# Moving the early routed rows' scatters to other places in GpSimd's program, in the last four passes of an audio tower kernel

## What is computed

```python
h = tok_ref(x, W, b)                           # signatures @ W.T + b
h = h + attn_ref(layernorm(h), ...)
h = h + ffn_ref(layernorm(h), ...)

def ffn_ref(x, gate_w, w1, w2, w3, sw1, sw2):  # D = 128, I = 512, E = 8, K = 1
    logits = xf @ gate_w.T
    wts, idx = top_k(logits, 1)
    comb = one_hot(idx) * softmax(wts)
    h = silu(xf @ w1[e].T) * (xf @ w3[e].T)    # of each expert e
    y = sum over e of (h * comb) @ w2[e].T
    return y + gelu(xf @ sw1.T) @ sw2.T
```

## Time and profile before

| | |
|---|---|
| median of 3 runs | 676.93 us (676.33 to 677.5) |
| profiled execution, whole | 676.65 us |
| its span | 674.8 us |
| TensorE (PE) busy | 638.4 us, 95% |
| VectorE (DVE) busy | 417.5 us, 62% |
| GpSimd (POOL) busy | 298.7 us, 44% |
| ScalarE (ACT) busy | 288.2 us, 43% |
| granted clock of TensorE, mean | 0.987 |

### The profile page before, as it was taken

The page is one execution under the profiler, slowest core; times in us unless marked ns, Lnnn a source line. Parts: engine busy times, 40 slices in busy tenths (PEclk is TensorE's granted clock), DMA queues, the critical chain, the costliest instruction groups (busy, mean ns, idle before and its releaser), DMA issues.

```text
span 674.8 us, 14377 instructions
## 1 busy us (share of the span) xinstructions
PE 638.4 (95%) x4237; PEld 539.0 (80%) x4270; DVE 417.5 (62%) x1073; ACT 288.2 (43%) x656; POOL 298.7 (44%) x336
## 2 busy tenths in 40 slices
PE   5989999999999999999999999999798999999994
PEld 3767888877888788887788887778577999999994
DVE  7966666666666666665666667776535354555534
ACT  3334444544445444445444454433374433444450
POOL 1355444545445454455444454445853213333330
PEclk9989999999999999999999999999988999999997
DMA  8511433534634434334343342112335211111108
GB/s 310 220 68 33 106 78 85 116 80 101 118 78 111 92 87 101 78 92 111 78 105 82 79 114 46 36 35 69 86 91 191 64 33 38 43 44 44 46 26 250
DMA packets 70006, 61.81 MB, mean 92 GB/s; under 512 B 6092, under 2 KB 58189, under 8 KB 69600
## 3 DMA queue, kind: packets, MB, share of 16 engines
q1 hardware_dynamic: 67712, 57.31, 33.6%
q0 software_dynamic: 2272, 4.22, 1.8%
HBM read 18.88 MB, written 26.30 MB: 67 GB/s over the span
## 4 chain that ended last, share of the span: by engine, by line
PE 81%; DVE 7%; issue 4%; POOL 3%; ACT 2%; DMA 1%; SPq 1%; DVEq 0%; POOLq 0%; ACTq 0%
PE bank L1256 74%; PE bank L1312 2%; PE bank L1465 2%; POOL sorted_rows L502 1%; POOL z L487 1%; DMA x<-expert_rows 1%; SPq L432 1%; PE bank L1556 1%; PE bank L1371 1%; PE bank L1362 0%; PE bank L1317 0%; POOL z L489 0%; PE bank L1316 0%; DMA sq<-square 0%; DVE utl L796 0%
## 5 line engine op out<-in xcount | busy, mean ns | idle before, releaser
L1256 PE MATMUL bank<-whigh,uth 128*128 128x512 f32 x512 | 168.8, 410 | 1.2 <-DVE lowt L796 1.2
L1256 PEld LDWEIGHTS bank<-whigh,uth 128*128 128x128 f32 x512 | 92.2, 190 | 28.0 <-issue 7.4
L1256 PE MATMUL bank<-whigh,utl 128*128 128x512 f32 x256 | 101.8, 398 | 0.0
L496 POOL TENSOR_TENSOR rstd<-rstd,powers 128x1 f32<-128x1 f32 x64 | 35.3, 551 | 119.9 <-DVE rstd L889 64.7
L487 POOL TENSOR_TENSOR z<-z 128x512 f32<-128x512 f32 x32 | 42.3, 1322 | 91.0 <-DVE z L902 91.0
L573 POOL DMA_INDIRECT expert_rows<-prob,ids x39 | 38.3, 983 | 89.2 <-ACT prob L750 89.2
L1256 PE MATMUL bank<-xvo,x 128*128 128x128 f32 x624 | 76.4, 276 | 0.7 <-issue 0.4
L1256 PEld LDWEIGHTS bank<-xvo,x 128*128 128x128 f32 x624 | 72.8, 192 | 1.4 <-issue 0.7
L1256 PE MATMUL bank<-xT,qkw 128*128 128x128 f32 x512 | 63.7, 278 | 0.0
L1256 PEld LDWEIGHTS bank<-xT,qkw 128*128 128x128 f32 x512 | 60.8, 195 | 0.1
L1256 PEld LDWEIGHTS bank<-whigh,utl 128*128 128x128 f32 x256 | 48.3, 189 | 11.9
(11 more groups left out here) (229 smaller groups left out, 1325.9 us busy)
## 6 DMA issues: line engine op xcount, KB each, us to landing
sorted_rows<-blank SPq DMA_DIRECT2D x24, 709.5 KB, 6.3
xvp<-xvo SPq DMA_DIRECT2D x128, 128.0 KB
w<-w_t SPq DMA_DIRECT2D x1, 4096.0 KB, 12.0
xvo<-sorted_rows SPq DMA_DIRECT2D x39, 64.5 KB, 1.9
w<-w_high SPq DMA_DIRECT2D x4, 512.0 KB, 6.8
x_columns<-x2t SPq DMA_DIRECT2D x32, 64.0 KB
xg_in<-x_columns SPq DMA_DIRECT2D x8, 256.0 KB
levels<-w_t SPq DMA_DIRECT2D x1, 2048.0 KB, 7.7
```

The source lines that it names most:

```text
L496: G.tensor_tensor(rstd[:, n, 1:2], rstd[:, n, 0:1], powers[:, 0:1], ALU.pow) \
L1256: return T.matmul(out_, lhsT, rhs, start=start, stop=stop)
```

## The change

The 24 early scatters are issued in the same order, at other places of POOL's program:

| place in POOL's program | before | after |
|---|---|---|
| pass 28, last | 0 to 2 | 0 to 2 |
| pass 29, between root(0, 30) and root(1, 28) | 3 to 5 | 3 to 5 |
| pass 29, between root(1, 28) and add_channels(31) | 6, 7 | 6 |
| pass 29, behind add_channels(31), ahead of root(0, 31) | 8 to 10 | 7 |
| pass 30, between root(0, 31) and root(1, 29) | 11 to 13 | 8 to 10 |
| pass 30, behind root(1, 29) | 14 to 19 | 11 to 16 |
| pass 31, behind root(1, 30), ahead of root(1, 31) | 20 to 23 | 17 to 19 |
| behind root(1, 31), ahead of the wait for pos_ready | none | 20 to 23 |

```diff
@@ in POOL's iteration(i, f, u, acc, prev) @@
                 if is_tile(i, SCATTER_AT + 1):
                     scatter(range(3, 6))
                 if is_tile(i, SCATTER_AT + 2):
-                    scatter(range(11, 14))
+                    scatter(range(8, 11))
                 if prev:
                     root(1, ln2, i - 1)
                 if is_tile(i, SCATTER_AT + 1):
-                    scatter(range(6, 8))
+                    scatter(range(6, 7))
                 if is_tile(i, SCATTER_AT + 2):
-                    scatter(range(14, 20))
+                    scatter(range(11, 17))
                 if is_tile(i, SCATTER_AT + 3):
-                    scatter(range(20, EARLY))
+                    scatter(range(17, 20))
                 if u:
                     add_channels(i + 2)
...
                 if is_tile(i, SCATTER_AT + 1):
-                    scatter(range(8, 11))
+                    scatter(range(7, 8))
...
             iteration(TILES - 1, False, False, False)
             root(1, ln2, TILES - 1)
+            scatter(range(20, EARLY))
```

## The result

| | before | after |
|---|---|---|
| first comparison: median (runs) | 676.63 us (4) | 671.38 us (4) |
| ratio, 95% interval | | 0.9924, 0.9906 to 0.9941 |
| two later comparisons, ratio and interval | | 0.9940 (0.9919 to 0.9961), 0.9934 (0.9913 to 0.9955) |
| profiled execution, span | 676.65, 674.8 us | 670.9, 669.1 us |

The change makes the kernel faster, by 5.1 us in the first comparison and 4.1 and 4.5 in the later ones (each ratio times 676).

The account below looks back on a forecast made before the run. Bound by TensorE nearly everywhere, with POOL's early scatters delaying work that DVE or PE awaits. Gains of 0.9, 0.6, 0.8 and 0.8 make 3.1 us: 676.65 - 3.1 = 673.55, put down as 673.6, range 671.8 to 675.2.

Parts of the forecast that it names:

- sum over channels of pass 29: Pass 29 on POOL: with scatter 7 behind it, the sum starts at 476.65 in place of 477.57; gain 0.9 us.
- xn of pass 30, to the softmax product: First norm of pass 30: DVE's 1.06 us wait for the root goes, but ACT's exponential limits the gain to 0.6.
- x2n of tile 29: Second norm of pass 30: the three scatters ahead of its root start sooner, so the root starts at once; gain 0.8.
- to x2n of tile 30, forecast by the clock near 490: Stretch near 490 where ACT is the bound: with an earlier clock fall gone, 0.1 to 0.2 us.
- x2n of tile 31: Last norm, pass 31: three scatters, not four, ahead of the root cut DVE's 1.47 us wait to 0.65; gain 0.8.
- up(2)'s clock: PE's shared-expert matmuls after two idle times: half clock there costs 1.58 us, which shorter gaps might save.
- A: Main case: gains as summed, clock falling again at up(2): 3.1 us, 673.6 (673.1 to 674.6); chance 0.47.
- B: Same gains, but shorter gaps leave the clock full before up(2): 3.1 + 1.6 = 4.7 us, 672.1; chance 0.31.
- the lower bound: Pass 29's sum: gain only 0.3 us if DVE's subtraction beside the sum goes first and holds POOL up.
- C: Pass 31: ACT or a transfer, such as head copies, holds its old time; gain 0.8 to 2.3 us; chance 0.12.
- D: What the roots gain is waited for elsewhere at once; time within 0.2%; chance 0.06.
- E: Slower: four late scatters meet w2's 2 MB load, group 4's columns come late and PE waits; 679 given; chance 0.04.

Follow-up runs that it names:

- e3: Kernel before, with two scatters moved from ahead of the root of pass 30's first norm to behind the root of its second: 673.27 us, ratio 0.9970.
- e4: Kernel before, with only scatter 23 moved behind the last root: 673.38 us, ratio 0.9966.
- e1: Control: the kernel before, unchanged, run again: 676.2 us, ratio 1.0007.
- e5: Kernel before, with only scatter 7 moved from ahead of the last sum over channels to behind it: 676.69 us, ratio 1.0009.
- e10: Kernel after plus 17 filling matmuls of no use in PE's two idle times, second run of that program: 670.20 us, ratio 0.9912 to before.
- e12: Kernel after, with eight scatters behind the last root in place of four: 672.38 us, ratio 0.9941 to before.
- e2: Control: the kernel after, unchanged, run again: 671.05 us, ratio 0.9940 to before.
- e9: The kernel after, unchanged, run a third time: 671.56 us, ratio 0.9934 to before.
- e6: Kernel after, with 16 scatters behind the last root in place of four, none in passes 30 and 31: 680.47 us, ratio 1.0069 to before.
- e11: Against e10: one scatter fewer ahead of root(0, 30), nine not six behind root(1, 29), two not four behind the last root: 670.51 us, ratio 0.9923 to before.
- e7: Kernel after plus 17 filling matmuls of no use in PE's two idle times: 670.24 us, ratio 0.9923 to before.
- e8: Kernel before plus 17 filling matmuls of no use in PE's two idle times: 673.43 us, ratio 0.9964.

## Why the prediction was right and wrong

**The mechanism of the scatters held in every step.** A scatter ahead of a due instruction on POOL is paid by DVE, or by PE through the sum. As the prediction put the steps, against the table (after against before):

| step | forecast | measured |
|---|---|---|
| sum over channels of pass 29 | 0.9 | 0.73 |
| xn of pass 30, to the softmax product | 0.6 | 0.62 |
| x2n of tile 29 | 0.8 | 0.82 |
| to x2n of tile 30, forecast by the clock near 490 | 0.1 to 0.2 (not in the 3.1) | 0.32 |
| x2n of tile 31 | 0.8 | 1.14 |
| in all at the last norm | 3.1 | 3.63 |
| up(2)'s clock | 0 (A) or 1.6 (B) | 0.13 or 1.55 |

The parts add up: at up(2) e3 is 1.82 and e4 1.18 ahead of e1, and with the sum's 0.75, which only counts once the root behind it is free too (e5), that makes 3.75; the whole change has 3.70. Of the 0.32 near 490 the clock is worth some 0.14: so much later is x2n of tile 30 in e10 and e12, where the clock fell near 488, than in e2 and e9, with x2n of tile 29 at the same place. The rest of it stays open.

**Pass 29 was nearly 0.2 short**, by the collision that was given as the lower bound: L489 took 1.27 us, where it took 1.07 before and takes 0.73 in the undisturbed pass 28, and DVE's L797 took 0.68 in place of its 1.33. They changed roles. The bound of 0.3 was too low because L489 had been 0.34 us long beside the same DVE instruction before as well. The Trainium skill has the rule that of a GpSimd instruction that reads SBUF and a DVE instruction with two SBUF inputs the one that starts first makes the other wait for its whole length ("SBUF — State Buffer", section "SBUF: two separate sides"). The rows agree: L797 starts at 477.05, L489 at 477.07.

**The last root was mis-sized**, 0.8 for 1.14: I read DVE's wait, 1.47 us, from one execution in which DVE was late too, behind the copies by head. The distance between two x2n that POOL's work sets, 5.67 us with four scatters, repeats to 0.01 and was the safer number. With DVE at its usual time the wait is 1.84 (e1), the gain 1.14.

**The clock was the step that failed.** I made A (the clock falls again at up(2), its term nothing) and B (it stays full, 1.6) two exclusive cases, A the likelier, and took A for the number. The same kernel does both: with idle times of 1.2 to 1.5 and 0.86 us ahead of up(2) the clock fell in three of seven profiles (after, e6, e12) and stayed in four (e2, e3, e4, e9); with 2.1 or 2.4 it fell in all three (before, e1, e5; in e5 later, and for 5.29 us of work where the others have 4.3 to 4.45). With the fills it stayed in all four. So the change takes away the fall in a part of its executions (two of the three profiles of the kernel after itself), and the median should lie between 3.8 and 5.2 less than before, where 4.1 to 5.1 was measured. How the missing 2 us of the first comparison divide is not shown. In the one profile it has of the kernel after the clock did fall, so A's term held there: of the 5.75 us between the two profiled executions 3.8 lie between the first scatter and the first expert, and 0.96 each ahead of pass 28 and in the experts' part, where the programs are the same. How often the clock fell in the other executions, and whether something lasting stands ahead of pass 28, stays open. The Trainium skill's sentence that activity lifts the throttled state ("TensorE: Matmul & The Clock Gate", "What's actually happening") pointed the right way; it was given 0.31.

**The range's low end** was 671.8, which is 5.1 below the 676.93 that the forecast started from. B with the true sizes is 5.2 less, and the median of before was 676.63 once a fourth run was in: 671.4, below the range. That the measured 671.38 agrees so well is luck: before itself had medians of 675.7, 675.75, 676.3 and 676.6 in four comparisons.

**Of the rivals**, C did not occur in this kernel (PE's wait of 0.3 for the head copies even went) but did in e11; D is out by e3 and e4; E, columns of group 4 that come late by the scatters' traffic, occurred at none of four, eight and sixteen late scatters. Sixteen are dear by another path, the late count of 32.

## What to carry to other kernels

When one in-order engine holds both bulk issues and tiny operations for which others wait, put the bulk behind the next due operation and count, place by place, how many fit before it is due; a move from one due operation to the next (e5) gains nothing. Size a wait by the distance between two starts on the engine that holds it, which repeats, and not by the idle time of the one that waits. Where TensorE has idle times near those that drop its clock, treat the clock's price as a share of executions and add that share to the sum.

## What the runs showed of the chip

- The granted clock of the same kernel with the same idle times (1.23 and 0.86 us) ahead of a stretch was half in one execution (after: 12 matmuls in 4.32 us) and full in two (e2, e9: 2.90 and 2.89). With matmuls of no use in the gaps it was full there in all four profiles (e7, e8, e10, e11).
- The same near 488, behind an idle time of 1.59 us without fills: half in e10, full in e7, one and the same program. There it cost 0.14 us and not 1.4, since ACT was the bound.
- One and the same program differed by up to 0.6 us ahead of the last passes and 1.4 in the routed experts' part from execution to execution (after, e2, e9).
- An indirect scatter of 128 rows holds POOL 1.26 us with its gap. Four copies by SP landed in 3.1 us (median) with scatters issued beside them (e11) and in 2.3 without (e2, e10, e12), and PE waited 0.92 us; that the scatters are the cause is argued.
- A stall of 4.07 us on PE, which put its next work 4.5 us late, cost 8.1 in the end (e6): 3.6 us arose behind the stall, in part by half clock.
